# A graph kernel: the turned heads' blocks pass through memory, and ScalarE makes the first network's exponentials before the turn

## The chip, the cores and the metric

The kernel runs on one core of one Trainium2 chip. A core has five engines that each work through their own queue in order: TensorE (PE; its weight loads are listed as PEld), VectorE (DVE), ScalarE (ACT), GpSimd (POOL) and SyncE (SP), which here only issues DMAs. They are tied together by semaphores. The metric is the device time of one execution in microseconds (us); smaller is better.

## What is computed

Sixteen graphs of 512 nodes with 256 features each pass through two attention networks over their adjacency matrix. Cut to what matters:

```python
# first network, three layers
scores = si[:, :, None] + sj[:, None, :] + attn_b[l]        # one head
scores = jnp.where(scores >= 0, scores, 0.2 * scores)
attn   = softmax(where(mask, scores, -inf), axis=-1)
h      = layernorm(x + attn @ x, g1, beta1)
x      = layernorm(h + gelu(h @ W1 + b1) @ W2 + b2, g2, beta2)
# second network, eight heads of 32 features
att    = softmax(where(A > 0, leaky_relu(a_src + a_dst + b_att), NEG_INF))
out    = relu(att @ xh)
# after each network: x = layernorm(x + network(x))
```

The probabilities come out with the target row on the partitions. To multiply them with the node features, TensorE needs the neighbours on the partitions: every 512x512 matrix of probabilities has to be turned.

## The kernel before, in words

All arithmetic is in float32. The work is a hand-ordered software pipeline. A unit is one layer of the first network for one graph; two graphs (a pair) alternate, so there are 8 pairs x 6 units = 48 units. The slot of a unit, 0 to 5, is its number modulo 6. While pair p runs through the first network, the 16 heads of pair p-1 are made in the gaps: slots 0 to 4 make three heads each and slot 5 one (`MADE_IN_SLOT`). In units 0 to 6 almost nothing of the second network is in the way; these and units 45 and 46 are called light below, units 7 to 44 busy.

In unit g the engines do the following.

- DVE ends the layer of unit g-1 (`layer_ends`), makes the scores' two sums for unit g+1 (`scores`), waits for TensorE to spread them over a row (`first_target_row`, L1087), adds the mask (`first_targets`, L749) and the row maxima, whose negative is `nm0` (L756). After that come `first_exponents` (L770), which adds `nm0` to the scores in place, head work (`head_targets`, `heads_out`), and then `attention`, which takes the products as TensorE ends them (L807, L809). After the attention come more head work, the bias, the two halves of `fed_forward` (L853), masks, and the end of the unit.
- PE does `first_product` f = 0 to 7 (L1198). f = 3 needs the second `fed_forward` of the unit before, and the spread row L1087 stands between f = 5 and f = 6. Then come pieces 0 to 3 of `second_product` (L1209), `attention` (turns L1108 by transposing into PSUM, products L1125), and pieces 6 to 15.
- ACT does the Gelu of each f (L518), the leaky ReLU of the first network's scores (`score0`, L487) after Gelu 6 and Gelu 7, then `probabilities` (L505): it reads the turned arguments out of PSUM and writes their exponential to SBUF. Gelu and Exp need different function tables, so a table load stands before each of the two groups.

A head of the second network (512x512 in the ring tile `prob1`) is turned in another way, for heads below `MOVED`: DVE transposes 32x32 blocks into the tile `blocks` (`turn_blocks`, L797), and SP copies the 16 pieces of 32 partitions x 512 elements to their new partitions with one DMA each (`move`, L361). There is one tile `blocks`, so the next `turn_blocks` waits until the copies of the last have landed. Four heads together are multiplied with their values by PE (`attend_heads`, L1150), copied out by ACT (`head_rows`, L523), transposed back by PE (`heads_back`, L1158) and scaled by DVE (`heads_out`, L897). In slots 0, 2 and 5 a finished four is taken ahead, between first_product and the pieces; in slot 3 it is taken among the pieces after the attention (`ahead` false). In busy units `turn_blocks` runs before the attention (slots 1 to 5), after it (slots 1 to 5) and at the end of the unit (all slots).

Of the kernel before, what the change touches and what calls it, by code (L numbers as in the profile page):

```python
# [6 lines left out]
F32 = mybir.dt.float32  # L7
# [125 lines left out]
def build(nc, x, adj, attn_w, attn_b, w1, b1, w2, b2, g1, beta1, g2, beta2, w_proj, w_att, b_att, out,  # L133
          scr_n, scr_t):
    ctx = ExitStack()
    with ctx:
# [97 lines left out]
        def sem(name):  # L234
            return ctx.enter_context(nc.semaphore(name))
# [14 lines left out]
        s_score0, s_arg, s_score1, s_exp = sem("score0"), sem("arg"), sem("score1"), sem("exp")  # L250


        s_block, s_moved = sem("block"), sem("moved")
        s_pt, s_prob, s_pd, s_copy = sem("pt"), sem("prob"), sem("pd"), sem("copy")
        s_av0, s_av0e = sem("av0"), sem("av0e")
        s_av1, s_oT, s_back, s_av1e = sem("av1"), sem("oT"), sem("back"), sem("av1e")
# [6 lines left out]

        s_passed = sem("passed")
        block = ctx.enter_context(nc.Block())
        rows_dram = nc.dram_tensor("rows_dram", (GRAPHS, HEADS, N), F32, kind="Internal").ap()

        def nodes(dram, graph):
# [25 lines left out]
        def _(sp):  # L294
# [60 lines left out]

            def move(q):

                sp.wait_ge(s_block, q + 1)
                for a in range(BLOCKS):
                    for b in range(BLOCKS):  # L360
                        sp.dma_start(ring(q)[b * BLOCK:(b + 1) * BLOCK, a, :],  # L361
                                     blocks[a * BLOCK:(a + 1) * BLOCK, b, :]).then_inc(s_moved, 16)

            stored, loaded = [0], [0]

# [113 lines left out]
        def _(act):  # L479
# [17 lines left out]
            def exponential(q, t):  # L497
# [2 lines left out]
                nc.scalar.activation(m, m, ACT.Exp, bias=nm1[:, q % RING, t:t + 1], scale=1.0,  # L500
                                     accum_out=sums[:, q % RING, t:t + 1]).then_inc(s_exp, 1)

            def probabilities(t):
                act.wait_ge(s_pt, c("pt"))
                nc.scalar.activation(prob0[:, t, :], pT[t % BANKS][:], ACT.Exp).then_inc(s_prob, 1)  # L505

            def turned_out(q, t):
                act.wait_ge(s_pt, c("pt"))
# [49 lines left out]
            for t in range(T):  # L558
                score0(0, t)
            for t in range(T):  # L560
                probabilities(t)
            normalise(ATTENDED, y_att, xs[0], s_hn)
            for dt in range(DT):
# [4 lines left out]
            for g in range(UNITS):  # L568
                p, s, l = unit_of(g)
                _, s2, l2 = unit_of(g + 1)  # L570
                new, heads = made(g), turned(g)
                place, four = side_by_side(heads)
                spent, ahead = spent_by(g)
                att = g + 1 < UNITS
                begin, ends = begun(g), first_ends(g)
                for f in range(FT):
                    gelu(l, f)
                    if f < T:
                        for q in held:
                            score(q, f)  # L580
                    else:
                        for q in heads[:1]:
                            turned_out(q, f - T)
                    if f >= FT - 2 and att:
                        score0(g + 1, 2 * (f - FT + 2))
                        score0(g + 1, 2 * (f - FT + 2) + 1)
                if spent is not None and ahead:
                    head_rows(spent)
                if not att:
                    first_network_out(ends)  # L590
                    for dt in range(DT):
                        state_out(GRAPHS - 2, dt)
                    for t in range(T):
                        values_out(GRAPHS - 2, t)
                    targets_out(GRAPHS - 2)
                    for t in range(T):
                        turned_out(heads[1], t)
                for t in range(T):
                    if att:
                        probabilities(t)  # L600
                    for q in held:
                        exponential(q, t)
                    for q in new[:1]:
                        score(q, t)
                if att and ends is not None and ends % 2 == 0:
                    first_network_out(ends)
                if g and first_ends(g - 1) is not None and first_ends(g - 1) % 2:
                    first_network_out(first_ends(g - 1))
                for q in new[:1]:
                    for t in range(T):  # L610
                        exponential(q, t)
                if place == 0:
                    head_rows(four)
                if att:
                    for t in range(T):
                        for q in heads[1:2]:
                            turned_out(q, t)
                        if begin is not None and t >= T - DT:
                            state_out(begin, t - T + DT)
                if att:  # L620
                    normalise(ATTENDED, y_att, xs[s2], s_hn)
                for t in range(T):
                    for q in heads[2:3]:
                        turned_out(q, t)
                    if begin is not None:
                        values_out(begin, t)
                    if t == 0 and place == 1:
                        head_rows(four)
                    if t == 0 and spent is not None and not ahead:
                        head_rows(spent)  # L630
                    if t == 1 and att:
                        for dt in range(DT):
                            transposed(dt, l2)
                for q in new[1:2]:
                    for t in range(T):
                        score(q, t)
                if begin is not None:
                    targets_out(begin)
                for q in new[1:2]:
                    if place == 2:  # L640
                        head_rows(four)
                    for t in range(T):
                        exponential(q, t)
                held = new[2:]
# [24 lines left out]
        def _(dve):  # L669
# [95 lines left out]
                maxima(col0[:], nm0[:]).then_inc(s_nm0, 1)  # L765
                dve.wait_ge(s_nm0, c("nm0"))

            def first_exponents(t):
                dve.wait_ge(s_score0, c("score0"))
                v.tensor_scalar(prob0[:, t, :], prob0[:, t, :], nm0[:, t:t + 1], None, ALU.add).then_inc(s_arg, 1)  # L770

            def head_targets(q, t):
                if t == 0:
                    dve.wait_ge(s_trow1[q % ROWS], 16 * (q // ROWS + 1))
# [17 lines left out]
            def turn_blocks(q):  # L792

                dve.wait_ge(s_exp, T * (q + 1))
                if q:
                    dve.wait_ge(s_moved, 16 * BLOCKS * BLOCKS * q)
                v.transpose(blocks[:].rearrange("p b (x i) -> p x b i", i=BLOCK),  # L797
                            ring(q)[:].rearrange("p t (j b i) -> p (t j) b i", b=BLOCKS, i=BLOCK)).then_inc(s_block, 1)

# [166 lines left out]
            dve.sem_inc(s_setup, 1)  # L966
            scores(0, 0)
            first_targets(0)
            for t in range(T):
                first_exponents(t)  # L970
            attention(0, 0)
            make_masks(1)

            for g in range(UNITS):
# [22 lines left out]
                for t in range(T):  # L997
                    for q in new[:1]:
                        head_targets(q, t)
                    if att and t < T // 2:  # L1000
                        first_exponents(2 * t)
                        first_exponents(2 * t + 1)
                for q in new[:1]:
                    head_maxima(q)
                if att:
# [71 lines left out]
        def _(pe):  # L1077
# [57 lines left out]
            def attend_heads(q):  # L1135

                by_act, by_vector = all_out.get((q + SIDE - 1, T - 1), (0, 0))
                if by_act:
                    pe.wait_ge(s_prob, by_act)
                if by_vector:  # L1140
                    pe.wait_ge(s_copy, by_vector)
                if q < MOVED:
                    pe.wait_ge(s_moved, 16 * BLOCKS * BLOCKS * min(q + SIDE, MOVED))
                pe.wait_ge(s_x1Te, turning[0])
                pe.wait_ge(s_rows, values[0])
                if spent[0]:
                    pe.wait_ge(s_av1e, spent[0])
                for j in range(T):
                    for i in range(SIDE):
                        last = te.matmul(av1[i * HD:(i + 1) * HD, :], xp[q // HEADS % 2][:, j, q % HEADS + i, :],  # L1150
                                         sources(q + i, j), start=j == 0, stop=j == T - 1)
                last.then_inc(s_av1, 1)
                spent[0] += 1
# [112 lines left out]
            for g in range(UNITS):  # L1266
# [49 lines left out]
                for t in range(T):  # L1316
# [4 lines left out]
                    piece(10 + t)  # L1321
                    if t == 0 and place == 1:
                        attend_heads(four)
                    if t == 0 and four_spent is not None and not ahead:
                        attend_heads(four_spent)
                    if t == 1 and att:
                        for dt in range(DT):
                            transpose_state(s2, dt)
                    if t == 2 and place == 1:
                        heads_back(four)  # L1330
                    if t == 2 and four_spent is not None and not ahead:
                        heads_back(four_spent)
                if place == 2:
                    attend_heads(four)
                piece(14)
                if begin is not None:
                    targets_in(begin)
                if place == 2:
                    heads_back(four)
                piece(15)  # L1340
            for h in range(LAST_HEADS - 1, GRAPHS * HEADS):
                n = h - LAST_HEADS
# [40 lines left out]
```

## Time and profile before

| | us |
|---|---|
| median of 3 runs (2542.44 to 2555.09) | 2545.91 |
| the profiled execution, its own time | 2541.38 |
| its span, first to last instruction | 2539.6 |
| PE busy, share of the span | 2208.2, 87% |
| DVE busy | 1940.8, 76% |
| ACT busy | 1570.7, 62% |
| mean granted TensorE clock | 0.951 |

Busy means that an instruction was running; ends of matmuls are modelled, so PE's share is somewhat too high. The span and the execution's own time differ by 1.8 us.

### The profile page before, as it was taken

The numbers are of one execution on the slowest core, as the hardware profiler recorded it, in microseconds if no ns is written. First come the engines' busy times: TensorE is split into PE (matmuls) and PEld (weight loads), VectorE is DVE, ScalarE is ACT, GpSimd is POOL, SyncE is SP. The second block draws the span as 40 slices with busy tenths as digits, with TensorE's granted clock in tenths as the row PEclk, the third lists the DMA queues.
The fourth block names the chain that finished last, engine by engine and source line by source line (L and its number), as shares of the span: only waits on it lengthen the run. The fifth ranks groups of instructions, "written<-read, shape, count | busy, mean of one in ns | idle before, by whom it ended". The sixth has DMA issues, their size and how long they took to land.

```text
span 2539.6 us, 31414 instructions
## 1 busy us (share of the span) xinstructions
PE 2208.2 (87%) x9537; PEld 1491.3 (59%) x9537; DVE 1940.8 (76%) x5778; ACT 1570.7 (62%) x3007; POOL 189.4 (7%) x200
## 2 busy tenths in 40 slices
PE   3999998888988888888998889988998988899866
PEld 2767675556556555655565556655665556667543
DVE  5555887877788787788868877788786887786587
ACT  2344576664766656665576656666566564768686
POOL 0001010001000010000100001000010000001000
PEclk9999999999999999999999999999999999999977
DMA  5001224334334343343343423434424333330111
GB/s 201 9 33 50 75 72 120 108 94 131 93 103 115 89 136 112 82 116 92 125 120 83 135 73 118 120 82 130 129 73 119 99 101 104 84 95 22 30 46 34
DMA packets 164118, 238.48 MB, mean 94 GB/s; under 512 B 30537, under 2 KB 79981, under 8 KB 163949
## 3 DMA queue, kind: packets, MB, share of 16 engines
q1 hardware_dynamic: 163948, 236.47, 32.3%
q8 instruction: 77, 1.26, 0.2%
q14 instruction: 93, 0.75, 0.1%
HBM read 120.74 MB, written 8.65 MB: 51 GB/s over the span
## 4 chain that ended last, share of the span: by engine, by line
DVE 35%; PE 29%; SPq 19%; ACT 6%; DMA 5%; issue 4%; POOL 1%; DVEq 0%; POOLq 0%; ACTq 0%
SPq L361 19%; DVE blocks L797 8%; PE ffn L1209 7%; PE av L1125 6%; DVE prob L749 5%; PE av L1198 5%; DVE prob L740 4%; DMA prob<-blocks 4%; PE ffn L1198 4%; DVE stats L688 3%; DVE xs L865 3%; DVE xs L859 2%; PE pT L1108 2%; PE av L1150 2%; ACT prob L487 2%
## 5 line engine op out<-in xcount | busy, mean ns | idle before, releaser
L1209 PE MATMUL ffn<-w_sb,G 128*128 128x256 f32 x3072 | 734.9, 383 | 0.0
L1209 PEld LDWEIGHTS ffn<-w_sb,G 128*128 128x128 f32 x3072 | 573.5, 192 | 106.4 <-issue 34.2
L1198 PE MATMUL ffn<-hT,w_sb 128*128 128x512 f32 x768 | 406.9, 668 | 115.7 <-DVE xs L853 114.6
L749 DVE CUSTOM_DVE_ANT_0 prob<-trow,mask 128x512 f32<-128x512 f32 x704 | 457.4, 686 | 44.4 <-DMA trow<-rows_dram 21.7
L1198 PE MATMUL av<-hT,w_sb 128*128 128x512 f32 x768 | 374.7, 623 | 0.0
L500 ACT ACTIVATE prob<-prob,nm 128x512 f32<-128x512 f32 x512 | 363.0, 712 | 0.0
L494 ACT ACTIVATE prob<-prob,s 128x512 f32<-128x512 f32 x512 | 350.4, 713 | 11.9 <-DVE nm L756 11.8
L1198 PEld LDWEIGHTS ffn<-hT,w_sb 128*128 128x128 f32 x768 | 161.9, 216 | 323.7 <-issue 210.0
L797 DVE STREAM_TRANSPOSE blocks<-prob 128x2048 f32<-128x2048 f32 x102 | 235.6, 2310 | 135.2 <-DMA prob<-blocks 135.2
L448 POOL TENSOR_TENSOR rstd<-veps,mhalf 128x4 f32<-128x4 f32 x127 | 160.0, 1260 | 2305.5 <-DVE veps L684 2305.5
L518 ACT ACTIVATE G<-av,cols 128x512 f32<-128x512 f32 x192 | 131.5, 685 | 259.4 <-PE av L1198 259.4
L518 ACT ACTIVATE G<-ffn,cols 128x512 f32<-128x512 f32 x192 | 131.2, 683 | 204.0 <-PE ffn L1198 202.7
L1198 PEld LDWEIGHTS av<-hT,w_sb 128*128 128x128 f32 x768 | 148.7, 199 | 171.1 <-issue 171.1
L1125 PE MATMUL av<-xs,prob 128*128 128x257 f32 x1024 | 245.0, 381 | 1.9 <-ACT prob L505 1.9
L1108 PE MATMUL pT<-ident,prob 128*128 128x128 f32 x1184 | 193.7, 292 | 48.2 <-DVE prob L802 19.6
L1108 PEld LDWEIGHTS pT<-ident,prob 128*128 128x128 f32 x1184 | 153.8, 150 | 95.7 <-issue 34.6
L1125 PEld LDWEIGHTS av<-xs,prob 128*128 128x128 f32 x1024 | 186.8, 190 | 27.8 <-ACT prob L505 4.7
L807 DVE RECIPROCAL small<-av 128x1 f32<-128x1 f32 x192 | 31.8, 165 | 214.1 <-PE av L1125 214.1
L534 ACT ACTIVATE xs<-prob,shift,rstd 128x256 f32<-128x256 f32 x192 | 99.6, 590 | 154.1 <-POOL shift L453 154.0
L505 ACT ACTIVATE prob<-pT 128x512 f32<-128x512 f32 x192 | 113.5, 591 | 97.9 <-PE pT L1108 96.7
L487 ACT ACTIVATE prob<-prob,small 128x512 f32<-128x512 f32 x192 | 127.4, 712 | 49.9 <-DVE small L756 49.8
L1125 PE MATMUL av<-xin,prob 128*128 128x257 f32 x512 | 123.0, 383 | 0.0
(120 smaller groups left out, 2461.1 us busy)
## 6 DMA issues: line engine op xcount, KB each, us to landing
prob<-blocks SPq DMA_DIRECT2D x1632, 64.0 KB, 2.0
w_sb<-in_L_gnn_W SPq DMA_DIRECT2D x48, 1024.0 KB, 7.5
trow<-rows_dram SPq DMA_DIRECT2D x128, 256.0 KB, 3.3
adj_sb<-in_adj SPq DMA_DIRECT2D x16, 1024.0 KB, 7.0
xin<-in_x SPq DMA_DIRECT2D x16, 512.0 KB, 6.2
x0r<-in_x SPq DMA_DIRECT2D x16, 512.0 KB, 4.4
out<-o SPq DMA_DIRECT2D x15, 512.0 KB, 3.0
aw_row<-in_L_gnn_attn_w SPq DMA_DIRECT2D x1, 768.0 KB
```

The source lines that it names most:

```text
L361: sp.dma_start(ring(q)[b * BLOCK:(b + 1) * BLOCK, a, :], blocks[a * BLOCK:(a + 1) * BLOCK, b, :]).then_inc(s_moved, 16)
L448: nc.gpsimd.tensor_tensor(rstd[which][:], veps[which][:], mhalf[:], ALU.pow).then_inc(s_rstd, 1)
L487: nc.scalar.activation(prob0[:, t, :], prob0[:, t, :], ACT.Prelu, bias=col0[:, t:t + 1], scale=1.0, alpha=SLOPE).then_inc(s_score0, 1)
L494: nc.scalar.activation(m, m, ACT.Prelu, bias=s1[q // HEADS % 2][:, t, q % HEADS:q % HEADS + 1], scale=1.0, alpha=SLOPE).then_inc(s_score1, 1)
L500: nc.scalar.activation(m, m, ACT.Exp, bias=nm1[:, q % RING, t:t + 1], scale=1.0, accum_out=sums[:, q % RING, t:t + 1]).then_inc(s_exp, 1)
L518: nc.scalar.activation(G[:, f, :], ff1[f % len(ff1)][:], ACT.Gelu, bias=b1_col[:, l, f:f + 1]).then_inc(s_gelu, 1)
L749: return v.tensor_tensor_reduce(out=out_[:, t, :], in0=targets, in1=mask[:, t, :], scale=1.0, scalar=LEAST, op0=ALU.add, op1=ALU.max, accu ...
L797: v.transpose(blocks[:].rearrange("p b (x i) -> p x b i", i=BLOCK), ring(q)[:].rearrange("p t (j b i) -> p (t j) b i", b=BLOCKS, i=BLOCK)) ...
L1108: last = te.transpose(pT[bank][:, j * P:(j + 1) * P], src[:, t, j * P:(j + 1) * P], ident[:])
L1125: last = te.matmul(av0[t % BANKS][:, 0:D + 1], prob0[:, t, j * P:(j + 1) * P], state(s, l)[:, j, :], start=j == 0, stop=j == T - 1)
L1198: last = te.matmul(ff1[f % len(ff1)][:], w1_sb[:, g // 2 % STAGES, dt, f * P:(f + 1) * P], hT[:, dt, :], start=dt == 0, stop=dt == DT - 1)
L1209: last = te.matmul(ffn[part][:, at:at + D], G[:, f, t * P:(t + 1) * P], w2_sb[:, g // 2 % STAGES, f, :], start=f == 0, stop=f == FT - 1)
```

## The change

It has three parts.

1. The turned blocks of a head no longer go straight to their new partitions. Four DMAs write `blocks` to a tensor in DRAM (semaphore `left`), SP waits for them, and a fifth DMA reads the head back as 128 rows. `turn_blocks` now waits for `left`, not for `moved`.
2. For the first network, ACT makes the exponential in SBUF with `nm0` as its bias (`exponential0`), ahead of the turn; what it does after the turn is a plain copy out of PSUM. DVE's `first_exponents` is gone.
3. In slot 3 the four that isn't ahead is multiplied after all of pieces 10 to 13, and its copy-out on ACT comes after the scores of the second new head.

```diff
+        blocks_dram = nc.dram_tensor("blocks_dram", (BANKS, BLOCKS, BLOCK, BLOCKS, N), F32, kind="Internal").ap()
             def move(q):
+                i = q % BANKS
                 sp.wait_ge(s_block, q + 1)
+                if q >= BANKS:
+                    sp.wait_ge(s_moved, 16 * (q - BANKS + 1))
                 for a in range(BLOCKS):
-                    for b in range(BLOCKS):
-                        sp.dma_start(ring(q)[b * BLOCK:(b + 1) * BLOCK, a, :],
-                                     blocks[a * BLOCK:(a + 1) * BLOCK, b, :]).then_inc(s_moved, 16)
+                    sp.dma_start(blocks_dram[i, :, :, a, :].rearrange("b j n -> j b n"),
+                                 blocks[a * BLOCK:(a + 1) * BLOCK, :, :]).then_inc(s_left, 16)
+                sp.wait_ge(s_left, 16 * BLOCKS * (q + 1))
+                sp.dma_start(ring(q)[:], blocks_dram[i].rearrange("b j a n -> (b j) a n")).then_inc(s_moved, 16)
...
+            def exponential0(u, t):
+                act.wait_ge(s_score0, T * u + t + 1)
+                nc.scalar.activation(prob0[:, t, :], prob0[:, t, :], ACT.Exp, bias=nm0[:, t:t + 1], scale=1.0).then_inc(s_arg, 1)
             def probabilities(t):
                 act.wait_ge(s_pt, c("pt"))
-                nc.scalar.activation(prob0[:, t, :], pT[t % BANKS][:], ACT.Exp).then_inc(s_prob, 1)
+                nc.scalar.copy(prob0[:, t, :], pT[t % BANKS][:]).then_inc(s_prob, 1)
...
+                for t in range(DT if att else 0):
+                    exponential0(g + 1, t)
                 for t in range(T):
                     if att:
                         probabilities(t)
+                    if att and t + DT < T:
+                        exponential0(g + 1, t + DT)
...
-            def first_exponents(t):
-                dve.wait_ge(s_score0, c("score0"))
-                v.tensor_scalar(prob0[:, t, :], prob0[:, t, :], nm0[:, t:t + 1], None, ALU.add).then_inc(s_arg, 1)
...
                 if q:
-                    dve.wait_ge(s_moved, 16 * BLOCKS * BLOCKS * q)
+                    dve.wait_ge(s_left, 16 * BLOCKS * q)
```

On ACT, in a busy unit of slot 1 (first the second score pair, then the attention's loop), the queue reads as follows; `prob` is the first network's tile, `prob_2` and `prob_3` are heads. Before:

```order
L487 ACTIVATE prob<-prob,small 128x512 x2
L505 ACT_TABLE_LOAD
L505 ACTIVATE prob<-pT 128x512
L500 ACTIVATE prob_2,sums<-prob_2,nm 128x512
L494 ACTIVATE prob_3<-prob_3,s_0 128x512
L505 ACTIVATE prob<-pT 128x512
```

Now, in the same unit:

```order
L492 ACTIVATE prob<-prob,small 128x512 x2
L510 ACT_TABLE_LOAD
L510 ACTIVATE prob<-prob,small 128x512 x2
L514 COPY prob<-pT 128x512
L510 ACTIVATE prob<-prob,small 128x512
L505 ACTIVATE prob_2,sums<-prob_2,nm 128x512
L499 ACTIVATE prob_3<-prob_3,s_0 128x512
L514 COPY prob<-pT 128x512
```

Two exponentials stand between the table load and the first copy out of PSUM, and one more behind each of the first two copies. The number of table loads in the whole queue is the same.

On SP, two heads in a row, before:

```order
L353 DMA trow<-rows_dram 128x512
L361 DMA prob_4<-blocks 32x512 x16
L353 DMA trow<-rows_dram 128x512
L361 DMA prob_5<-blocks 32x512 x16
L353 DMA trow<-rows_dram 128x512
```

and now:

```order
L354 DMA trow<-rows_dram 128x512
L364 DMA blocks_dram<-blocks 32x4x512 x4
L367 DMA prob_4<-blocks_dram 128x2048
L354 DMA trow<-rows_dram 128x512
L364 DMA blocks_dram<-blocks 32x4x512 x4
L367 DMA prob_5<-blocks_dram 128x2048
```

Sixteen issues became five, with a wait in front of the fifth.

On PE in slot 3, after the attention (L1209 and L1215 are the pieces, L1185 and L1191 the transposed state, L1158 and L1164 `heads_back`), before:

```order
L1209 MATMUL ffn<-w_sb,G 128x256 x10
L1150 MATMUL av<-prob_4,xp 32x512
...
L1150 MATMUL av<-prob_7,xp 32x512
L1209 MATMUL ffn<-w_sb,G 128x256 x2
L1185 MATMUL av_0<-ident,xs 128x128 x4
L1185 MATMUL av_1<-ident,xs 128x128 x4
L1209 MATMUL ffn<-w_sb,G 128x256 x2
L1158 MATMUL av<-ident,prob_7 128x128 x4
```

and now:

```order
L1215 MATMUL ffn<-w_sb,G 128x256 x12
L1191 MATMUL av_0<-ident,xs 128x128 x4
L1191 MATMUL av_1<-ident,xs 128x128 x4
L1215 MATMUL ffn<-w_sb,G 128x256 x4
L1156 MATMUL av<-prob_4,xp 32x512
...
L1156 MATMUL av<-prob_7,xp 32x512
L1215 MATMUL ffn<-w_sb,G 128x256 x2
L1164 MATMUL av<-ident,prob_7 128x128 x4
```

The 16 head products moved behind the transposed state and two more pieces.

## Rows read from the trace of the kernel before

**Rows 1.** The page: busy time, and the last chain's shares by engine.
```profile
PE 2208.2 (87%) x9537; PEld 1491.3 (59%) x9537; DVE 1940.8 (76%) x5778; ACT 1570.7 (62%) x3007; POOL 189.4 (7%) x200
DVE 35%; PE 29%; SPq 19%; ACT 6%; DMA 5%; issue 4%; POOL 1%; DVEq 0%; POOLq 0%; ACTq 0%
```

**Rows 2.** Waits of the span: who for whom, us in total, times, longest.
```profile
DVE blocks L797 <- DMA prob<-blocks: 135.2, 53, 7.9
...
PE ffn L1198 <- DVE xs L853: 114.6, 36, 5.8
```

**Rows 3.** The same wait in units 31 to 35 (slots 1 to 5), one row each.
```profile
DVE blocks L797 <- DMA prob<-blocks: 8.7, 2, 7.7
...
DVE blocks L797 <- DMA prob<-blocks: 3.6, 1, 3.6
...
DVE blocks L797 <- DMA prob<-blocks: 2.4, 2, 2.0
...
DVE blocks L797 <- DMA prob<-blocks: 2.8, 2, 1.7
...
DVE blocks L797 <- DMA prob<-blocks: 4.9, 2, 3.3
```

**Rows 4.** Timeline of DVE, end of unit 31: start, us, instruction, idle before.
```profile
1592.62 2.31 DVE L797 STREAM_TRANSPOSE blocks<-prob 128x2048 f32<-128x2048 f32 x1 [0.92 <-DMA prob<-blocks]
...
1607.36 2.31 DVE L797 STREAM_TRANSPOSE blocks<-prob 128x2048 f32<-128x2048 f32 x1 [7.75 <-DMA prob<-blocks]
```

**Rows 5.** Timeline of PE, from the end of unit 31 on.
```profile
1602.31 1.88 PE L1198 MATMUL ffn<-hT,w_sb 128*128 128x512 f32 x4
1604.03 3.60 PE L1198 MATMUL av<-hT,w_sb 128*128 128x512 f32 x8
...
1610.30 5.40 PE L1198 MATMUL ffn<-hT,w_sb 128*128 128x512 f32 x8 [2.67 <-DVE xs L853]
...
1618.83 0.65 PE L1087 MATMUL trow<-ident,raw 128*128 128x128 f32 x4 [1.41 <-DVE raw L740]
```

**Rows 6.** Timeline of PE and then of ACT in a light unit (unit 4).
```profile
226.26 0.60 PE L1087 MATMUL trow<-ident,raw 128*128 128x128 f32 x4
...
233.59 0.60 PE L1108 MATMUL pT<-ident,prob 128*128 128x128 f32 x4
...
233.16 1.28 ACT L505 ACT_TABLE_LOAD   x1
234.46 0.60 ACT L505 ACTIVATE prob<-pT 128x512 f32<-128x512 f32 x1
```

**Rows 7.** Timeline of a busy unit of slot 4 (unit 22), PE and ACT.
```profile
1115.98 1.28 ACT L505 ACT_TABLE_LOAD   x1
...
1117.22 0.60 PE L1108 MATMUL pT<-ident,prob 128*128 128x128 f32 x4
```

**Rows 8.** Timeline of a busy unit of slot 2 (unit 32), ACT and PE.
```profile
1627.15 1.28 ACT L505 ACT_TABLE_LOAD   x1
...
1630.41 0.60 PE L1108 MATMUL pT<-ident,prob 128*128 128x128 f32 x4
```

**Rows 9.** Groups: line, engine, shapes, count | busy, mean ns | idle before.
```profile
L487 ACT ACTIVATE prob<-prob,small 128x512 f32<-128x512 f32 x192 | 127.4, 712 | 49.9 <-DVE small L756 49.8
...
L770 DVE TENSOR_SCALAR prob<-prob,small 128x512 f32<-128x512 f32 x192 | 91.5, 485 | 24.6 <-ACT prob L487 13.8
```

**Rows 10.** The copies of one head on SP's queue.
```profile
1120.36 10.02 SPq L361 DMA_DIRECT2D prob<-blocks  x16
```

**Rows 11.** DMA issues: count, KB each, median us from issue to landing.
```profile
prob<-blocks SPq DMA_DIRECT2D x1632, 64.0 KB, 2.0
...
out<-o SPq DMA_DIRECT2D x15, 512.0 KB, 3.0
...
out<-o SPq DMA_DIRECT2D x2, 256.0 KB, 2.1
```

**Rows 12.** Landing of the 1024 KB loads of L299.
```profile
DMA to landing us min/median/max: 5.2/7.0/11.4
```

More of the change, by code:

```diff
@@ L250, in build @@
         s_score0, s_arg, s_score1, s_exp = sem("score0"), sem("arg"), sem("score1"), sem("exp")
-        s_block, s_moved = sem("block"), sem("moved")
+        s_block, s_left, s_moved = sem("block"), sem("left"), sem("moved")
         s_pt, s_prob, s_pd, s_copy = sem("pt"), sem("prob"), sem("pd"), sem("copy")
@@ L560, in _ @@
             for t in range(T):
+                exponential0(0, t)
+            for t in range(T):
                 probabilities(t)
@@ L628, in _ @@
                         head_rows(four)
-                    if t == 0 and spent is not None and not ahead:
-                        head_rows(spent)
                     if t == 1 and att:
@@ L638, in _ @@
                     targets_out(begin)
+                if spent is not None and not ahead:
+                    head_rows(spent)
                 for q in new[1:2]:
@@ L968, in _ @@
             first_targets(0)
-            for t in range(T):
-                first_exponents(t)
             attention(0, 0)
@@ L999, in _ @@
                         head_targets(q, t)
-                    if att and t < T // 2:
-                        first_exponents(2 * t)
-                        first_exponents(2 * t + 1)
                 for q in new[:1]:
@@ L1142, in attend_heads @@
                 if q < MOVED:
-                    pe.wait_ge(s_moved, 16 * BLOCKS * BLOCKS * min(q + SIDE, MOVED))
+                    pe.wait_ge(s_moved, 16 * min(q + SIDE, MOVED))
                 pe.wait_ge(s_x1Te, turning[0])
@@ L1323, in _ @@
                         attend_heads(four)
-                    if t == 0 and four_spent is not None and not ahead:
-                        attend_heads(four_spent)
                     if t == 1 and att:
@@ L1330, in _ @@
                         heads_back(four)
-                    if t == 2 and four_spent is not None and not ahead:
-                        heads_back(four_spent)
                 if place == 2:
                     attend_heads(four)
+                if four_spent is not None and not ahead:
+                    attend_heads(four_spent)
                 piece(14)
@@ L1339, in _ @@
                     heads_back(four)
+                if four_spent is not None and not ahead:
+                    heads_back(four_spent)
                 piece(15)
```

## The prediction

> **What bounds the kernel now.** I read the page first. PE is busy 87%, DVE 76%, ACT 62%, and the last chain is 35% DVE, 29% PE and 19% SP's queue [rows 1]: no engine alone. The list of waits says how they interlock. DVE stands 135.2 us, 53 times, until the copies of a head have landed, and PE stands 114.6 us at the start of units until DVE has added the second half of the feed-forward sum (L853) [rows 2]. So a DVE that is late ends the unit, and some of its lateness is the wait for the tile `blocks`.
>
> The end of unit 31 shows it. DVE starts `turn_blocks` at 1607.36 after 7.75 us of idleness and has it done at 1609.67 [rows 4]. PE had begun the next unit at 1602.31, ran f = 0 to 2, and continues at 1610.30, when L853 is done [rows 5]; L853 takes the 0.65 us between. From there it takes DVE 8.5 us to the sums that PE spreads over a row at 1618.83, for which PE waits again, 1.41 us [rows 5]. I read a unit as a loop of three pieces: (a) end of L853 to the spread row, 8.5 us, DVE's; (b) spread row to the first turn and through the attention, PE's or ACT's; (c) from there to the next end of L853, DVE's in most units. All the waits for `blocks` lie in (c), behind or at the end of the attention.
>
> **Part 1, the move: the wait.** One head's copies take SP 10.02 us for 16 issues, 0.63 each [rows 10], and the last lands 2.0 us after its issue [rows 11]: 11.4 us from the end of a `turn_blocks` until `blocks` is free and the head complete. Now four issues take 2.5 us at the same price. The trace has no SBUF-to-DRAM write of 2 KB rows in this shape. Its nearest are the results: 256 KB land in 2.1 us, 512 KB in 3.0 [rows 11]. The last write then lands 4.0 to 4.9 us after the transpose (1.9 us for the first three issues, plus 2.1 to 3.0). By the rate of the 1024 KB loads, 5.2 us at best and 7.0 in the median [rows 12], it is 5.2 to 7. I take 4.9, nearest to the writes, and keep 4 to 7. The fifth DMA reads 1024 KB: 5.2 to 7. So `blocks` is free after 4.9 instead of 11.4 us, and the head is complete after about 4.9 + 0.5 + 5.2 = 10.6, not later than now.
>
> The Trainium skill (DMA: Bandwidth & Descriptors, Anatomy of one DMA) speaks against such a detour: each DMA has some 2 us of fixed cost, most of it the receipt of the last write, worst for HBM, and here two hops pay it in sequence. This case's rows show no dearer receipt for DRAM, 2.1 us against 2.0. By its fit (2 us plus bytes over 436 GB/s), as an estimate, each 1 MB hop is 4.4 us, which changes nothing below.
>
> How close are the next transposes? The tightest place is slot 1: in unit 31 one ends at 1592.62 + 2.31 = 1594.93 and the next could start at 1607.36 - 7.75 = 1599.61 [rows 4], 4.7 us later. A landing after 4.9 us costs 0.2 there, and slot 1 has 1.7 us of slack against PE (below). In the other slots the waits are at most 4.9 us [rows 3], so that 11.4 - 4.9 = 6.5 us or more lie between. SP is held in `move` for about 5.5 us, less than the 10 of now, so what is queued behind it (target rows, weights, adjacency) isn't later. PE needs a head's last piece at `attend_heads`, in the tightest case (slots 0 and 2) at the spread row plus two first products of 1.72 us [rows 5], that is 0.65 + 8.5 + 0.5 + 3.4 = 13.0 us after the transpose; 10.6 is in time, with 2.4 us to spare.
>
> **What the vanished waits are worth.** The five units of one pair with waits have 8.7, 3.6, 2.4, 2.8 and 4.9 us, together 22.4 [rows 3]; 135.2 is 6.04 such pairs. In slots 2 to 5 PE has less to do behind the attention than in slot 1 (no projection), or DVE has more (masks, a graph's end), so I let (c) shrink by all of it. In slot 1 it can't: PE reaches the next unit at 1602.31 [rows 5], so L853 can't end before 1602.31 + 0.2 + 0.65 = 1603.2, a gain of 7.0 instead of 8.7. And then PE has six first products of 1.72 us, 10.3 us, before the spread row, which comes at 1612.7 and not at 1603.2 + 8.5 = 1611.7. That takes 1.0 more: slot 1 gains 6.1 (1618.83 - 1612.7), the pair 6.1 + 3.6 + 2.4 + 2.8 + 4.9 = 19.8, and all pairs 19.8 x 6.04 = **120 us**.
>
> **Part 2, the exponentials.** ACT gets 192 more activations of 712 ns [rows 9], DVE loses 192 of 485 ns, 91.5 us, and 24.6 us of waits around them. I count neither as such. What DVE had to do ahead of the attention was waiting for PE anyway, in slots 0, 2 and 5, where PE works a four of heads first; the other slots gain at most the 0.3 us by which the attention took longer where a transpose preceded it. But piece (b) gets longer where PE has no four to do. In the light unit the table load ends at 234.44, and PE turned at 233.59 [rows 6]; now an exponential stands between them, and the turn can start at 234.44 + 0.71 + 0.1 = 235.25, **1.7 us later**. In the busy unit 22 it is 1117.26 + 0.71 + 0.1 = 1118.07 against 1117.22 [rows 7], 0.85 us later, as PE's clock was at its lower level there. In slot 2 the load ends at 1628.43 and the turn is at 1630.41 [rows 8]: 2 us, and the exponential fits in. So slots 0, 2 and 5 pay nothing, slots 1, 3 and 4 pay 0.85 to 1.7 less up to 0.3, about 1.1 each: 3.3 x 6.04 = **20 us**. The nine light units pay 1.7 each, **15 us**, the prologue 2. In the loop, ACT's longest round grows from about 1.8 to 2.4 us in the first two of four rounds, against PE's 2.2 per round; the third round catches up. I take 0, with the whole 0.6 per unit (28 us) as the bad end.
>
> There is a rule that would make this dearer. The row shows the load taking 1.28 us and the next activation 0.02 us behind it (234.46) [rows 6]. The Trainium skill (ScalarE: Activation LUTs, What ACT_TABLE_LOAD costs) counts 1.28 us plus a drain of 1.38 for each change of set; by it the path would carry 1.4 us more in 28 units. The row has no such drain, so I keep 1.28.
>
> **Part 3, the four of slot 3.** Work only changes places: the state is turned earlier, the heads later. There DVE makes masks, so it, not PE, ends the unit, and it wants the result late. 0; if PE became the later one, up to 1 us in 6 units.
>
> **The sum.** 120 - 20 - 15 - 2 = 83 us less. The profiled execution took 2541.4, so 2458; the median of before lies 4.5 above it, and I add most of that: **2462 us**.
>
> **Rivals.**
> - *DVE's shed work counts as well.* DVE has the largest share of the chain [rows 1]. If the attention starts on DVE's time after all, up to 91.5 + 24.6 = 116 us [rows 9] come on top, and ACT's delay is not paid. Half of it already gives 2404; all of it 2346. Against it: PE is what DVE's attention waits for. Chance 0.12.
> - *ACT is the late one in more places.* The loop costs its 0.6 us in all 47 units (28 us), or the drain above is real (1.4 x 28 = 39 us, by the skill's rule, chance 0.04 of this): 2490 to 2530. ACT's share rises from 62% to 67%, and its rounds in the attention come to be longer than PE's. Chance 0.18.
> - *The writes land late (slower).* Mechanism: four 2 KB-row writes to DRAM, each from 32 partitions, run below the rate of the loads, so `turn_blocks` waits as before, while ACT's 37 us are paid. At 11.4 us all 53 waits are back: 2541 + 37 = 2578. Since the average wait is 2.6 us, most are back by 10 us, and the point from which the kernel is slower is about 10.5 us. The rows give 4 to 7. Chance 0.07.
> - *The read-back lands late.* Above 13.0 us for both hops PE waits at `attend_heads` in 12 units, 1 us each per us: at 16 us, 35 us lost, 2497. Chance 0.07.
>
> **How the numbers follow.** The forecast has 0.56; its own range is 2435 to 2490 (writes at 7 us: +10; a loop at half its price: +14; half-clock stretches that vanish with PE's idleness, or appear: 15 either way). From 2415 to 2520 I leave out the larger part of the first rival and the slow case. Measurement can tell about 0.5%, 13 us. Faster 0.89, same 0.04, slower 0.07.
>
> **What would show it.** The wait DVE <- DMA at `turn_blocks` falls from 135 to under 20 us. SP has 408 writes and 102 reads; the last write lands about 5 us after the transpose. The 114.6 us of PE on L853 fall by half or more. Busy DVE falls by 91 us, busy ACT rises by 137. In light units the first turn is 9.0 us behind the spread row instead of 7.3 (233.59 - 226.26) [rows 6], and these units are 1.7 us longer. Units of slot 0 keep their length. I am wrong if DVE waits as long for `left`, if the light units don't grow, or if slot 0 gets shorter.

## The result and the profile after

The changed kernel takes 2467.5 us (median of 4, 2463.07 to 2468.74) against 2545.7 us, a ratio of 0.968 with a 95% interval of 0.966 to 0.971: 78 us faster. The forecast was 2462.

The page of the changed kernel, the same parts as [rows 1]:

```profile
PE 2175.5 (88%) x9537; PEld 1475.2 (60%) x9537; DVE 1852.0 (75%) x5586; ACT 1686.9 (68%) x3199; POOL 189.4 (8%) x200
...
PE 45%; DVE 39%; ACT 8%; issue 4%; DMA 2%; POOL 1%; SPq 0%; DVEq 0%; POOLq 0%; ACTq 0%
```

SP's queue had 19% of the last chain and now has none. PE has the largest share, and ACT has gone from 6% to 8%. The waits that answer to [rows 2], and those that grew:

```profile
DVE small L818 <- PE av L1131: 350.8, 192, 9.1
...
PEld pT L1114 <- ACT prob L510: 51.0, 29, 6.8
PE pT L1114 <- ACT prob L510: 39.4, 29, 6.4
PE ffn L1204 <- DVE xs L864: 34.7, 27, 3.2
...
DVE blocks L808 <- DMA blocks_dram<-blocks: 10.5, 7, 2.4
```

The wait for `blocks` fell from 135.2 us to 10.5 us, and PE's wait for the second half of the feed-forward sum (L853, now L864) from 114.6 to 34.7. A new line is PE's turn (L1114) waiting 39.4 us for ACT's exponential (L510). DVE's wait for PE at the attention (L818) is long: here lies the time that DVE saved. Before, the same wait was shorter by 137 us:

```profile
DVE small L807 <- PE av L1125: 214.1, 176, 3.6
```

The groups for the two kinds of work on ACT now, the exponential and the copy out of PSUM, beside [rows 9]:

```profile
L510 ACT ACTIVATE prob<-prob,small 128x512 f32<-128x512 f32 x192 | 133.4, 719 | 0.6
...
L514 ACT COPY prob<-pT 128x512 f32<-128x512 f32 x192 | 110.6, 577 | 55.3 <-PE pT L1114 51.0
```

The end of unit 31, which [rows 4] show before. DVE's two transposes and, from SP's queue, the transfers between them:

```profile
1549.14 2.31 DVE L808 STREAM_TRANSPOSE blocks<-prob 128x2048 f32<-128x2048 f32 x1
...
1557.49 2.31 DVE L808 STREAM_TRANSPOSE blocks<-prob 128x2048 f32<-128x2048 f32 x1 [1.37 <-DMA blocks_dram<-blocks]
```

```profile
1551.48 2.71 SPq L364 DMA_DIRECT2D blocks_dram<-blocks  x4
1557.42 0.34 SPq L367 DMA_DIRECT2D prob<-blocks_dram  x1
```

The first transpose ends at 1551.45. SP issues the read as soon as all four writes have landed, so the start of L367 is the time at which `blocks` is free: 5.97 us later. Over all 102 heads that distance is 6.0 us in the median. Before, the last of the 16 copies had landed 11.6 us after the transpose in the median: 9.45 us passed until the last issue began, the rest until all had landed. Where 7.75 us were lost, 1.37 are now. The two transfers by themselves:

```profile
blocks_dram<-blocks SPq DMA_DIRECT2D x408, 256.0 KB, 4.2
prob<-blocks_dram SPq DMA_DIRECT2D x102, 1024.0 KB, 4.8
```

And the light unit 4, beside [rows 6]: PE from the spread row (L1093) to the first turn (L1114), then ACT.

```profile
234.35 0.60 PE L1093 MATMUL trow<-ident,raw 128*128 128x128 f32 x4
...
243.32 0.66 PE L1114 MATMUL pT<-ident,prob 128*128 128x128 f32 x4 [1.48 <-ACT prob L510]
```

```profile
241.25 1.28 ACT L510 ACT_TABLE_LOAD   x1
242.54 1.33 ACT L510 ACTIVATE prob<-prob,small 128x512 f32<-128x512 f32 x2
```

The first exponential starts 0.01 us behind the table load, and the turn when it has ended: 8.97 us after the spread row, against 7.33.

To see where the time went I cut each trace at the end of the second L853 of each unit (or the line that answers to it) and took means by slot. The light units here are 1 to 6, 45 and 46. Columns: three kernels of the experiments stand beside before and after.

| mean us per unit | before | move alone | exponentials alone | parts 1 and 3 | after |
|---|---|---|---|---|---|
| light (8) | 42.0 | 42.0 | 43.5 | 42.0 | 43.7 |
| slot 0 (6) | 49.7 | 49.2 | 50.5 | 48.9 | 49.6 |
| slot 1 (7) | 50.0 | 43.4 | 50.3 | 43.5 | 44.5 |
| slot 2 (7) | 50.9 | 48.1 | 52.1 | 48.2 | 48.1 |
| slot 3 (6) | 49.9 | 48.9 | 50.0 | 49.2 | 50.1 |
| slot 4 (6) | 49.7 | 46.8 | 50.1 | 47.1 | 48.5 |
| slot 5 (6) | 54.1 | 49.9 | 53.3 | 49.3 | 49.6 |

Each column is one execution. Two executions of the move alone differ by up to 0.6 us in a slot's mean (slot 5: 49.9 and 49.3), so a smaller difference in a single slot says little.

### The profile page after: what moved, and what is told of

Same layout as the page of the kernel before. It is cut to its first block, busy times and chain, and to the rows that moved or that the text cites. A ratio compares the mean times of both kernels' runs of the same rounds, so it can differ in the third digit from the quotient of the medians.

```text
span 2464.9 us, 30392 instructions
## 1 busy us (share of the span) xinstructions
PE 2175.5 (88%) x9537; PEld 1475.2 (60%) x9537; DVE 1852.0 (75%) x5586; ACT 1686.9 (68%) x3199; POOL 189.4 (8%) x200
## 4 chain that ended last, share of the span: by engine, by line
PE 45%; DVE 39%; ACT 8%; issue 4%; DMA 2%; POOL 1%; SPq 0%; DVEq 0%; POOLq 0%; ACTq 0%
PE av L1131 14%; PE ffn L1215 11%; DVE prob L764 6%; PE av L1204 5%; PE pT L1114 5%; DVE prob L755 4%; PE ffn L1204 4%; DVE blocks L808 4%; DVE stats L703 3%; PE av L1156 3%; DVE xs L876 3%; ACT prob L492 3%; DVE xs L870 3%; DVE xs L864 2%; DVE xs L856 1%
## 5 line engine op out<-in xcount | busy, mean ns | idle before, releaser
L1215 PE MATMUL ffn<-w_sb,G 128*128 128x256 f32 x3072 | 734.9, 383 | 0.0
L1215 PEld LDWEIGHTS ffn<-w_sb,G 128*128 128x128 f32 x3072 | 572.9, 192 | 106.3 <-issue 34.2
L764 DVE CUSTOM_DVE_ANT_0 prob<-trow,mask 128x512 f32<-128x512 f32 x704 | 451.3, 685 | 42.1 <-DMA trow<-rows_dram 18.4
L1204 PE MATMUL ffn<-hT,w_sb 128*128 128x512 f32 x768 | 366.8, 611 | 35.8 <-DVE xs L864 34.7
L818 DVE RECIPROCAL small<-av 128x1 f32<-128x1 f32 x192 | 32.3, 168 | 350.8 <-PE av L1131 350.8
L1204 PEld LDWEIGHTS ffn<-hT,w_sb 128*128 128x128 f32 x768 | 148.9, 197 | 219.6 <-issue 187.2
L1114 PE MATMUL pT<-ident,prob 128*128 128x128 f32 x1184 | 194.2, 292 | 83.7 <-ACT prob L510 39.4
L808 DVE STREAM_TRANSPOSE blocks<-prob 128x2048 f32<-128x2048 f32 x102 | 235.5, 2309 | 11.0 <-DMA blocks_dram<-blocks 10.5
L1114 PEld LDWEIGHTS pT<-ident,prob 128*128 128x128 f32 x1184 | 151.1, 149 | 139.6 <-ACT prob L510 51.0
L492 ACT ACTIVATE prob<-prob,small 128x512 f32<-128x512 f32 x192 | 127.3, 712 | 41.1 <-DVE small L771 41.0
L514 ACT COPY prob<-pT 128x512 f32<-128x512 f32 x192 | 110.6, 577 | 55.3 <-PE pT L1114 51.0
L510 ACT ACTIVATE prob<-prob,small 128x512 f32<-128x512 f32 x192 | 133.4, 719 | 0.6
```

The costliest lines, as they stand in the source:

```text
L492: nc.scalar.activation(prob0[:, t, :], prob0[:, t, :], ACT.Prelu, bias=col0[:, t:t + 1], scale=1.0, alpha=SLOPE).then_inc(s_score0, 1)
L510: nc.scalar.activation(prob0[:, t, :], prob0[:, t, :], ACT.Exp, bias=nm0[:, t:t + 1], scale=1.0).then_inc(s_arg, 1)
L764: return v.tensor_tensor_reduce(out=out_[:, t, :], in0=targets, in1=mask[:, t, :], scale=1.0, scalar=LEAST, op0=ALU.add, op1=ALU.max, accu ...
L1114: last = te.transpose(pT[bank][:, j * P:(j + 1) * P], src[:, t, j * P:(j + 1) * P], ident[:])
L1204: last = te.matmul(ff1[f % len(ff1)][:], w1_sb[:, g // 2 % STAGES, dt, f * P:(f + 1) * P], hT[:, dt, :], start=dt == 0, stop=dt == DT - 1)
L1215: last = te.matmul(ffn[part][:, at:at + D], G[:, f, t * P:(t + 1) * P], w2_sb[:, g // 2 % STAGES, f, :], start=f == 0, stop=f == FT - 1)
```

## The experiments

My theory was that of the prediction: the move through DRAM gives some 120 us because `blocks` is free sooner, the exponentials on ACT cost about 37 us where ACT stands between the spread row and the first turn, and the moved four is worth nothing. The first rival: DVE's shed work is part of the gain. The others: the cost on ACT lies in the attention's loop of every unit, or the writes land late.

### The three parts alone

`e1_move_only` has part 1 alone: the kernel before with the new `move` and its semaphores.

> The kernel before with part 1 alone: heads' blocks through DRAM, exponentials and the four of slot 3 as before. My theory (the 120 us come from DVE's waits for the tile blocks, and ScalarE's exponentials cost 37): 2545 - 120 = 2425 to 2440, faster than the changed kernel by 25 to 40 us; the wait for the copies under 20 us, DVE's busy time as before. Rival (DVE's shed work counts as well): 2480 or more, slower than the changed kernel.

Measured: 2416.59 us, ratio 0.949 (0.947 to 0.952). That is 131 us less than the kernel before on that chip (2547.42), and **51 us less than the changed kernel** (on another chip; 42 on one and the same, below). The move by itself gains more than the whole change, and more than I expected: the time lies below my 2425 to 2440. By the profiles' spans the gain is 2539.6 - 2422.7 = 117 us; the profiled execution was the slowest of its four.

`e2_exponentials_only` has part 2 alone.

> The kernel before with part 2 alone. My theory: slower than before by 20 + 15 + 2 = 37 us, 2575 to 2590; light units 1.7 us longer each; DVE's waits for the copies about as before. Rival (DVE's shed work counts): faster than before, down to 2430.

Measured: 2572.46 us, ratio 1.010 (1.007 to 1.012), 25 us slower and just below the 2575 to 2590 that I expected; the light units grew by 1.4 us, not 1.7. DVE's wait for `blocks`, which I had expected to stay about as before, says why the delay costs so little:

```profile
DVE blocks L803 <- DMA prob<-blocks: 95.5, 35, 7.9
```

It was 135.2 us. While the first turn comes later, the copies go on; 40 us of the wait vanish, and pay a part of the delay. In slots 3 and 4 the units grow by 0.2 and 0.4 us only, though the turn is 2.2 and 1.7 us later there.

`e3_four_only` has part 3 alone, `e4_move_and_four` parts 1 and 3.

> The kernel before with part 3 alone, the four of slot 3 taken later. My theory: within 6 us of before, since DVE ends that unit. Rival (PE's early stop for a four whose last head hasn't landed cost time): up to 15 us faster.

> Parts 1 and 3 without the exponentials. My theory: as the kernel with part 1 alone within 5 us, 2425 to 2440, and the fastest of all. Rival: slower than the changed kernel for want of DVE's time.

Measured: 2547.22 us, ratio 1.0003 (0.999 to 1.0015), and 2424.59 us, ratio 0.952 (0.950 to 0.954). Part 3 does nothing that can be told from noise, alone or behind the move. Against the latter, part 2 costs 2467.5 - 2424.6 = 43 us, not 25: with the quick move there are no waits left that would hide it.

### What makes the move quick

`e5_sixteen_writes` keeps the way through DRAM and goes back to 16 issues; the semaphore's counts follow.

```diff
                 for a in range(BLOCKS):
-                    sp.dma_start(blocks_dram[i, :, :, a, :].rearrange("b j n -> j b n"),
-                                 blocks[a * BLOCK:(a + 1) * BLOCK, :, :]).then_inc(s_left, 16)
+                    for b in range(BLOCKS):
+                        sp.dma_start(blocks_dram[i, b, :, a, :],
+                                     blocks[a * BLOCK:(a + 1) * BLOCK, b, :]).then_inc(s_left, 16)
```

> The changed kernel with sixteen writes of 64 KB per head to DRAM in place of four of 256 KB, then the same read of 1 MB. The bytes and the memory are the same; only the number of issues is that of the kernel before. Theory (the number of issues on SP's queue sets when `blocks` comes free): 16 x 0.63 us and a landing make it 11.5 us again, the head is complete only after about 17 us, so DVE waits for `left` some 135 us in all, with longest waits of 7 to 8 us, and PE waits at `attend_heads` in 12 units up to 4 us each: 2467 + 123 to 131 (what the move had gained) + up to 45 = 2590 to 2640. Rival (it is the way through DRAM, or the larger pieces, that made it quick, whatever the number): 2467 to 2490, with waits under 20 us.

Measured: 2503.26 us, ratio 0.982 (0.981 to 0.984), 36 us slower than the changed kernel, and neither theory's number. The number of issues matters, but each issue is cheaper here than I took it. In the middle of the kernel:

```profile
1554.71 8.38 SPq L365 DMA_DIRECT2D blocks_dram<-blocks  x16
1564.38 0.34 SPq L368 DMA_DIRECT2D prob<-blocks_dram  x1
```

In the median of all heads 16 issues take 7.43 us, 0.46 each, where the same 16 pieces sent to SBUF took 10.02, 0.63 each. `blocks` is free after 9.1 us, not 11.5, and DVE waits 40.6 us, not 135:

```profile
DVE blocks L809 <- DMA blocks_dram<-blocks: 40.6, 13, 5.4
```

Beside `e2_exponentials_only`, which also issues 16 times but straight to SBUF, this kernel is 69 us faster (2572 against 2503): the cheaper issues alone free `blocks` 2.5 us earlier, 9.1 us after the transpose instead of 11.6. Four issues for sixteen free it 3.1 us earlier still and are worth the other 36 of 105 us. No run sends four larger DMAs straight to SBUF, so it isn't shown that the way through DRAM is needed.

`e7_written_twice` writes each head to two places.

```diff
-                for a in range(BLOCKS):
-                    sp.dma_start(blocks_dram[i, :, :, a, :].rearrange("b j n -> j b n"),
-                                 blocks[a * BLOCK:(a + 1) * BLOCK, :, :]).then_inc(s_left, 16)
+                for r in range(2):
+                    for a in range(BLOCKS):
+                        sp.dma_start(blocks_dram[i + r * BANKS, :, :, a, :].rearrange("b j n -> j b n"),
+                                     blocks[a * BLOCK:(a + 1) * BLOCK, :, :]).then_inc(s_left, 16)
```

> The changed kernel with every head written twice to DRAM (eight writes of 256 KB instead of four), so that `blocks` comes free later by four issues. Theory (what counts is the time until the last write has landed, against a gap of 4.7 us in slot 1 and of 6.5 us and more elsewhere): four more issues of 0.4 to 0.6 us make it 1.6 to 2.5 us later, slot 1 waits 1.4 + 2 us and mostly within PE's slack of 1.7 us, slots 2 and 5 some 0 to 1.5 us: DVE's wait for `left` rises from 10.5 to 25 to 50 us, and the time by 10 to 30 us, to 2477 to 2497. Rival (the writes are hidden as they stand, with room to spare): the wait under 20 us and 2467 within 5. Rival (the engines of the DMA are the limit, so that twice the bytes take twice the time, about 8 us or more): wait over 60 us, 2510 or more.

Measured: 2536.82 us, ratio 0.996 (0.994 to 0.997), 69 us slower than the changed kernel. The time is that of the last rival named there (2510 or more); DVE's wait, 52.1 us, is not, it lies just above my own 25 to 50. Eight writes free `blocks` after 10.1 us in the median, four after 6.0: 4.1 us for 1 MB more, 256 GB/s, where I had taken 1.6 to 2.5 for the issues. So what limits these writes is more than the price of an issue, most likely the transfer: the fourth issue of a head lasts 1.24 us already, the first 0.32. The read comes later too, and the wait for it of PE's weight loads, 6.0 us in the changed kernel, now counts:

```profile
DVE blocks L809 <- DMA blocks_dram<-blocks: 52.1, 13, 6.1
...
PEld av L1157 <- DMA prob<-blocks_dram: 36.1, 13, 4.5
PE av L1157 <- DMA prob<-blocks_dram: 25.3, 10, 3.7
```

Cut by slots as above, the units of slot 1 are 3.8 us longer than in the changed kernel (DVE's wait), those of slot 2 5.4 us (4.2 of it between the spread row and the first turn, where PE waits for the head's read, 2.7 us in the mean) and those of slot 0 1.1 us: 7 x 3.8 + 7 x 5.4 + 6 x 1.1 = 71 us. This is also the prediction's rival of the late read: the head is complete after 15.1 us, 2.1 above the 13.0 of the working, and at 1 us each in 12 units that rival gives 25 us, which is what PE waits. The kernels with part 2, ordered by when `blocks` is free (6.0, 9.1, 10.1 and, in `e2_exponentials_only`, 11.6 us), take 2467, 2503, 2537 and 2572 us. That is not the price of a late `blocks` alone, since the head is complete after 10.9, 14.2, 15.1 and 11.6 us.

### Where the exponentials cost

`e8_dve_work_back` puts DVE's load back, and no dependence: four operations that multiply constant tiles by 1, at the place of `first_exponents`.

```diff
+            def work_back(t):
+                m = aw_row[:, t, :, :].rearrange("p a d -> p (a d)") if t < LAYERS else be2_row[:, 0:2, :].rearrange("p a d -> p (a d)")
+                v.tensor_scalar(m, m, 1.0, None, ALU.mult).then_inc(s_dch, 1)
+                c.skip("dch")
...
+                    if att and t < T // 2:
+                        work_back(2 * t)
+                        work_back(2 * t + 1)
```

> The changed kernel with four VectorE operations of 512 elements put back per unit where `first_exponents` stood. They multiply constant tiles by 1, and nothing waits for them, so they only occupy VectorE, about 0.45 us each, 85 us in all. Theory (VectorE's shed work was worth nothing, since it waits for TensorE there): 2467 within 5, ratio to the kernel before as for the changed kernel, 0.968. Rival 1 of the prediction (the shed work counts): 85 us or half of that more, 2510 to 2550. In between, 5 to 20 us more, if the two operations behind the second head tile delay `turn_blocks` or the row maxima of a head.

Measured: 2467.59 us, ratio 0.968 (0.967 to 0.970), the same as without. The page and the wait show where it went:

```profile
PE 2173.2 (88%) x9537; PEld 1473.0 (60%) x9537; DVE 1916.3 (78%) x5774; ACT 1687.6 (68%) x3199; POOL 189.6 (8%) x200
...
DVE small L823 <- PE av L1139: 305.8, 187, 9.5
```

DVE is 64 us busier, of the 89 that it had shed, and waits 45 us less for PE; nothing shows in the time. The first rival falls.

`e9_three_slots` is the move alone, with ACT's early exponentials only where PE works a four of heads before the attention; `e10_other_units` is its complement. Elsewhere both keep DVE's `first_exponents` and the exponential behind the turn.

```diff
+def early_exponentials(g):
+    return 7 <= g <= 44 and g % SLOTS in (0, 2, 5)
...
+                early = early_exponentials(g)
+                for t in range(DT if early else 0):
+                    exponential0(g + 1, t)
                 for t in range(T):
                     if att:
-                        probabilities(t)
+                        probabilities(t, early)
+                    if early and t + DT < T:
+                        exponential0(g + 1, t + DT)
```

> The move alone (as in e1_move_only), and ScalarE makes the first network's exponentials ahead of the turn only in the busy units whose slot is 0, 2 or 5, where TensorE first works a four of heads; in all other units the exponential is made after the turn and VectorE adds nm0, as before. Theory (the exponentials cost only where ScalarE is waited for at the first turn: slots 1, 3, 4 and the light units): nothing is lost against e1_move_only, ratio 0.949 within 0.003, 2412 to 2424. Rival (the longer rounds of ScalarE in the attention's loop cost 0.6 us in every unit that has them): 19 units x 0.6 = 11 us more, 2428, ratio 0.954. Rival (VectorE's shed work is worth something in these slots): below 2410.

> The complement of e9_three_slots: the move alone, and ScalarE's exponentials ahead of the turn in the light units and the busy units of slots 1, 3 and 4, while slots 0, 2 and 5 keep the order of before. Theory (here ScalarE stands between the spread row and the first turn, so these units pay all of part 2): by the unit tables of the changed kernel against e4_move_and_four, 1.6 us in each light unit, 1.1 in slot 1, 0.9 in slot 3, 1.4 in slot 4, together 35 to 40 us on top of the move alone: 2450 to 2465, ratio 0.963 to 0.968. Rival (the cost lies in every unit alike, about 0.9 us): 28 of 47 units, 25 to 28 us, 2442 to 2445.

Measured: 2418.82 us, ratio 0.949 (0.948 to 0.950), and 2462.55 us, ratio 0.967 (0.965 to 0.970). In slots 0, 2 and 5 the exponentials on ACT cost nothing, and gain nothing; made only in the light units and slots 1, 3 and 4 they cost 39 us, where they cost 42 when made in all (both against the move alone on the same chip, next). So it is the first turn that costs, and not the loop, which is about equally long in every unit (below).

### The better kernel

> The move alone once more, on the chip on which the changed kernel also runs again: is it really the faster of the two? Theory: 2412 to 2424, ratio 0.949, 45 to 52 us below the changed kernel.

> The changed kernel once more, beside the move alone on the same chip: 2463 to 2470, ratio 0.968.

Measured on one chip with `e10_other_units`: 2423.61 us, ratio 0.951 (0.948 to 0.953), and 2465.74 us, ratio 0.968 (0.966 to 0.970). The move alone beats the changed kernel by 42 us, a little less than the 45 to 52 expected. No other kernel here beats it; `e9_three_slots`, at 2418.82 us, is its equal.

## Why the prediction was right, and where its terms were off

- **The wait of DVE at `turn_blocks`** (135 to under 20): right, 10.5. The last write was to land 4.9 us after the transpose, with 4 to 7 as bounds; it was 6.0. I had added one landing to three issues, as if the four writes didn't hold each other up; written twice they show 1.0 us for each further 256 KB. The 11.4 us taken for the way before is 11.6. In slot 1 DVE waits 1.4 us and not 0.2, but as the slack of 1.7 us said, little of it reaches the unit. The head is complete after 10.9 us in the median instead of 10.6, below the 13.0 at which PE needs it.
- **120 us for the vanished waits**: right. It is 131 and 126 us by the medians of the two runs of the move alone, 117 and 115 by the spans against that of [rows 1]. By slot, expected against measured: slot 1, 7.0 and 6.6; slot 2, 3.6 - 1.0 = 2.6 and 2.8; slot 4, 2.8 and 2.9; slot 5, 4.9 and 4.2. The 1.0 is the spread row of the next unit, which now waits for PE's six first products; it came as 0.7. **Slot 3** was mis-sized: 2.4 taken, 0.9 measured. Behind the first turn these units are 2.3 us shorter, as taken, but 1.4 came back between the spread row and the first turn (why, below). Slot 0, for which I had nothing, gained 0.5.
- **20 + 15 + 2 us for ACT's exponentials**: right, 42 to 43 behind the quick move. The 1.7 us per light unit came as 1.7. The 1.1 taken for slots 1, 3 and 4 is 1.0, 0.9 and 1.4 (last column of the table less the one before it). What I had left out is slot 0: 0.5 to 0.8 us, by the run compared with, 3 to 5 us in all. It isn't the exponentials of that slot, since `e10_other_units`, which makes none there, has the same 49.6 and `e9_three_slots` 49.1. In three of its six units the stretch from the spread row to the first turn takes 13.3 us at a mean granted clock of 0.87, in the other three 11.6 at 1.00, as in all six with parts 1 and 3. What pulls the lower level there stays open. The sum can't be made of the parts alone, though: -131 and +25 would be -106, the change gave -78. That the total came so close is in part luck: the move gave 6 to 11 us more than I took by the medians, and the exponentials cost 5 more, which partly cancels. My working priced part 2 as it stands behind part 1, which is why it came out. That 25 us of the cost were hidden as long as DVE waited for `blocks` anyway, I hadn't seen.
- **0 for the attention's loop**: nearly so. In the changed kernel it takes 10.6 to 10.8 us in the mean of any slot, with the move alone 10.6 to 10.9.
- **0 for DVE's shed work** and **0 for part 3**: both shown, the former by `e8_dve_work_back` and `e9_three_slots`.
- **The price of late writes**, in the third rival: too steep. By 10 us most of the waits were to be back; with `blocks` free after 10.1 us (`e7_written_twice`) DVE waits 52 us of the 135. That this kernel is nearly as slow as before all the same comes in good part from PE's wait for the late read, the fourth rival.
- **The drain and the two hops.** By the Trainium skill (ScalarE: Activation LUTs, What ACT_TABLE_LOAD costs) a change of table carries a drain of 1.38 us as well. The exponential 0.01 us behind the load shows none on this path. By the Trainium skill (DMA: Bandwidth & Descriptors, Anatomy of one DMA) a DMA takes 2 us plus its bytes over 436 GB/s, which gave the estimate of 4.4 us per hop of 1 MB; the section fits this to DMAs that GpSimd issues, and these are SP's. The read took 4.8 us, and the four writes 6.0. Two hops, 10.9 us to the complete head, are no slower here than the direct way, 11.6 us, of which 9.45 passed before the last issue; and `blocks` is free after the first hop.
- **The signs.** DVE busy fell by 89 us (91 expected), ACT rose by 116 (137 expected: the durations add up to 141 more, but neighbours overlap by 0.1 us, as in 1.33 us for two of 0.72), PE's wait on L853 fell by 70%, slot 0 kept its length.

In profiles, the change came to 2464.9 - 2539.6 = -75 us and was to be -83: 3 to 5 us less from the waits, 5 more for the exponentials, most of it in slot 0.

## What to carry to other kernels

A buffer that is freed by a transfer costs the time from the last write into it to the last landing; when that time is mostly issues on one queue, fewer and larger DMAs shorten it, even by way of memory and a second hop. Here a third of the gain came with the number (36 of 105 us) and the rest with issues that are cheaper on this way, and the 256 KB writes already held each other up. Price every part of a change on top of the others: what is hidden behind a wait that another part removes will be paid. And work moved from an engine that waits gains nothing, and costs wherever the engine that gets it is the one waited for: nothing in slots 0, 2 and 5, 39 us in the rest. Here part 2 should be left out.

## What the runs showed of the hardware

In slot 3 TensorE's granted clock decided where an idleness was paid. In unit 33 the kernel before waited 4.76 us for L853, and the move alone waits 1.04 us there but 3.11 us later, before the spread row. PE in this unit, before and then with the move alone, and behind it the granted clock (column PEclk) in the stretches around the two spread rows:

```profile
1661.55 5.40 PE L1198 MATMUL ffn<-hT,w_sb 128*128 128x512 f32 x8 [4.76 <-DVE xs L853]
1666.79 1.88 PE L1198 MATMUL av<-hT,w_sb 128*128 128x512 f32 x4
1670.08 0.65 PE L1087 MATMUL trow<-ident,raw 128*128 128x128 f32 x4 [1.41 <-DVE raw L740]
1670.57 1.88 PE L1198 MATMUL av<-hT,w_sb 128*128 128x512 f32 x4
1672.28 1.88 PE L1198 MATMUL ffn<-hT,w_sb 128*128 128x512 f32 x4
```

```profile
1576.96 3.70 PE L1203 MATMUL ffn<-hT,w_sb 128*128 128x512 f32 x8 [1.04 <-DVE xs L858]
1580.50 1.88 PE L1203 MATMUL av<-hT,w_sb 128*128 128x512 f32 x4
1585.49 0.65 PE L1092 MATMUL trow<-ident,raw 128*128 128x128 f32 x4 [3.11 <-DVE raw L745]
1585.97 2.89 PE L1203 MATMUL av<-hT,w_sb 128*128 128x512 f32 x4
1588.65 2.62 PE L1203 MATMUL ffn<-hT,w_sb 128*128 128x512 f32 x4
```

```profile
core 0: us, PE busy (x) PEld busy (x) DVE busy (x) ACT busy (x) POOL busy (x), PEclk, DMA share, GB/s
1662.20:1669.00 6.80, 6.46 (x12) 2.34 (x10) 6.37 (x27) 2.28 (x4) 1.17 (x1) 0.79 0.41 104
1670.10:1677.50 7.40, 7.40 (x29) 5.03 (x30) 6.87 (x19) 3.77 (x6) 0.00 (x0) 1.00 0.11 27
```

```profile
1577.60:1582.50 4.90, 4.78 (x12) 1.80 (x10) 4.55 (x16) 3.08 (x6) 1.17 (x1) 1.00 0.80 197
1585.60:1589.50 3.90, 3.90 (x9) 1.77 (x10) 3.83 (x11) 0.60 (x1) 0.00 (x0) 0.64 0.23 95
```

PEclk is the third number from the end: 0.79 and 1.00 before, 1.00 and 0.64 with the move alone, each a mean of the two levels (1.2 and 2.4 GHz). Before, the lower level fell into the products ahead of the spread row, where PE is early anyway: it waits 1.41 us more for the row. With the move alone it falls behind the spread row, on the way to the first turn, which in five of the six units of slot 3 comes 8.8 to 9.1 us after the spread row instead of 7.4. The mean is 8.7, so 1.4 of the 2.3 us that went behind the first turn are taken back. I had allowed for this as plus or minus 15 us, without a place.

The other surprise is the price of an issue: 0.63 us on SP's queue for a 64 KB piece to SBUF, 0.46 for the same piece to DRAM, 0.68 on the average for one of the four 256 KB writes (2.71 us), and 0.34 for the 1 MB read (L367).
